# A graph network on one core: four chunks to a PSUM bank in the table products, and the last dense layers as one pipeline over groups of 512 nodes

## What is computed

```python
h = jnp.maximum(_layernorm(x, axis=-1), 0.0)
# the fourth layer, with x standing for h
h = jnp.concatenate([x[row], edge_attr], axis=1)
h = jax.nn.relu(h @ W1a + b1a) @ W1b + b1b
sums = jax.ops.segment_sum(h, col, num_segments=n_nodes)
counts = jax.ops.segment_sum(jnp.ones((h.shape[0],), dtype=h.dtype), col, num_segments=n_nodes)
agg = sums / jnp.clip(counts, 1.0)[:, None]
z = jnp.concatenate([x, agg, u[batch]], axis=1)
return jax.nn.relu(z @ W2a + b2a) @ W2b + b2b
```

## Time and profile before

| | us |
|---|---|
| median of 3 runs | 9367.44 (9365.83 to 9368.25) |
| the profiled execution, as timed | 9366.17 |
| its span | 9364.40 |

### The profile page before, as it was taken

One profiled execution on the slowest core, in us unless ns is written; L12 is line 12 of the kernel. 1 busy time (PEld: TensorE's weight loads), 2 busy tenths in 40 slices (PEclk: granted clock), 3 DMA queues, 4 the chain that ended last, 5 costly groups with the idle time before them and its releaser, 6 DMA issues. The chain is left out here.

```text
span 9364.4 us, 133857 instructions
## 1 busy us (share of the span) xinstructions
PE 7028.5 (75%) x35740; PEld 4596.9 (49%) x35792; DVE 5660.6 (60%) x16783; ACT 2515.7 (27%) x5863; POOL 2656.2 (28%) x2952
## 2 busy tenths in 40 slices
PE   4777777775566659940488699999998777777787
PEld 4555555453122224420477544444445666666676
DVE  6777777775589990059899800000014777777786
ACT  0222222222467740020388600000001333310001
POOL 0777777776470000000000000000002444444410
PEclk9767776766679989975799899999999999999998
DMA  3333333334975538849566478787886766642363
GB/s 99 103 103 105 105 104 103 105 105 167 393 231 164 168 114 306 299 195 426 205 215 216 144 262 276 262 287 256 295 284 200 181 180 179 179 111 63 63 178 88
DMA packets 969628, 1759.77 MB, mean 188 GB/s; under 512 B 102288, under 2 KB 665125, under 8 KB 905315
## 3 DMA queue, kind: packets, MB, share of 16 engines
q1 hardware_dynamic: 683820, 1335.73, 44.1%
q0 software_dynamic: 110720, 276.01, 9.0%
q10 hardware_dynamic: 174394, 139.51, 5.5%
HBM read 1412.04 MB, written 338.80 MB: 187 GB/s over the span
## 5 line engine op out<-in xcount | busy, mean ns | idle before, releaser
L768 POOL DMA_INDIRECT bucketed<-arena,wide x1563 | 1515.6, 970 | 726.5 <-issue 714.0
L1920 PE MATMUL psum<-wide,arena 128*128 x6496 | 1209.9, 329 | 400.5 <-DVE arena L1979 393.9
L1920 PEld LDWEIGHTS psum<-wide,arena 128*128 128x128 f32 x6496 | 989.9, 195 | 618.3 <-issue 493.3
L1787 POOL DMA_DIRECT2D table<-wide x13 | 9.7, 743 | 4316.2 <-DVE wide L1711 4316.2
L1979 DVE TENSOR_SCALAR arena<-wide,tile_first 128x128 f32 x3248 | 870.8, 300 | 472.3 <-PE psum L1920 293.8
L1841 POOL DMA_INDIRECT arena<-table,src_i x832 | 803.3, 966 | 1009.1 <-PE psum L1937 872.4
L1660 PE MATMUL psum<-arena,h 128*128 128x512 f32 (+1 forms) x2548 | 1048.6, 570 | 19.1 <-DMA arena<-adjacency 17.5
L922 PE MATMUL psum<-arena 128*128 128x512 bf16 x2253 | 695.7, 442 | 435.0 <-DVE arena L870 259.4
L665 PE MATMUL psum<-arena 128*113 128x177 bf16 x1568 | 534.4, 341 | 416.2 <-ACT wide L687 374.6
L870 DVE TENSOR_SCALAR arena<-sums 128x512 bf16<-128x512 int16 x2304 | 799.9, 347 | 0.0
L659 PE MATMUL psum<-w_edge,arena 128*128 128x256 f32 x1568 | 786.9, 597 | 0.0
(11 more groups left out here) (398 smaller groups left out, 11006.0 us busy)
## 6 DMA issues: line engine op xcount, KB each, us to landing
arena<-adjacency SPq DMA_DIRECT2D x294, 1024.0 KB
arena<-adjacency SPq DMA_DIRECT2D x98, 1568.0 KB, 7.8
adjacency<-wide SPq DMA_DIRECT2D x588, 256.0 KB
arena<-adjacency SPq DMA_DIRECT2D x196, 640.0 KB, 3.9
arena<-adjacency SPq DMA_DIRECT2D x147, 768.0 KB
arena<-bucketed POOLq DMA_DIRECT2D x208, 528.0 KB, 6.0
arena<-adjacency SPq DMA_DIRECT2D x49, 1792.0 KB, 6.9
arena<-adjacency SPq DMA_DIRECT2D x49, 1344.0 KB, 6.1
```

What stands on the lines that cost most here:

```text
L768: e.indirect_dma_start(bucketed, bass.IndirectOffsetOnAxis(ap=places[k][0:size, c:c + 1], axis=0), rows[k][0:size, c, :], None).then_inc(s ...
L1920: e.matmul(flat[:, ds((chunk & 3) * 512 + 2048, P)], lhsT=hot[:, i % 8, :], rhs=table_in[:, ds(tile * P, P)], start=False, stop=True, skip ...
```

## The change

1. **Split.** `NEAR_PAIRS` goes from 416 to 320, so far pairs from 416 to 512. `LOOKS` is 3048; a round has six lookups (`PER_PAIR`), and 508 of the 512 far pairs have one.
2. **Banks.** A PSUM bank holds four near chunks side by side, a quad; four banks hold sixteen chunks. ScalarE prepares and evicts a quad with one instruction each, 512 wide. Hots have sixteen slots. Sources are loaded eight chunks at a time.
3. **Rings.** Far gathers and far edge loads have four slots (`FAR`) instead of eight, the near block's loads four instead of eight.
4. **Tail inputs.** The third convolution also stores the turned nodes to DRAM (`nodes_t`), thirteen more transfers on GpSimd's queue. A row of flags, which node has an edge, is stored early. Both are fetched back (3.2 MB each into SBUF) on ScalarE's queue in the near block.
5. **Tail.** The three dense layers and the store are one pipeline over thirteen groups of 512 nodes (the last has 128). TensorE turns only the means; the first two layers' products have the weights as the stationary side and 512 columns of nodes. `b1b` and the flags are applied in one VectorE instruction, the rectifier reads PSUM and takes its bias on ScalarE, and each group is stored when its sum is ready.
6. The fold of `u` into the bias moves to the small steps behind the early scatter.

The core of the diff:

```diff
-NEAR_PAIRS = PAIRS // 2
+NEAR_PAIRS = 320
 NEAR = NEAR_PAIRS * PAIR
 FAR_PAIRS = PAIRS - NEAR_PAIRS
-LOOKS = -(-(NEAR + BUCKETS_49 + 2) // 16) * 16
+PER_PAIR = 6
+LOOKS = -(-(NEAR + BUCKETS_49 + 2) // PER_PAIR) * PER_PAIR
 MARKS = -(-LOOKS // P) * P
 NEAR_BLOCKS = -(-NEAR // P)
 DUMP = 4096
 PACK = 4096
 EARLY, LATE = 2560, 512
-PER_PAIR = 8
 QUAD = 4
+HOTS = 16
+FAR = 4
+NEAR_BANKS, ROW_QUADS, EDGE_QUADS = 4, 8, 3
+LIST_FROM = ROW_QUADS * QUAD
...
                             e.dma_start(table_nodes[:, a // P:(a + n) // P, :], wide2[:, a // P:(a + n) // P, :]).then_inc(s_saved, 16)
-                        e.wait_ge(s_saved, 16 * GROUPS)
+                            e.dma_start(nodes_t[:, a:a + n], part(wide, a, n)).then_inc(s_saved, 16)
+                        e.wait_ge(s_saved, 32 * GROUPS)
...
-            ring = slots(PAIR * P, DEEP).rearrange("p k (c w) -> p k c w", c=PAIR)
-            edge_in = slots(PAIR * P, DEEP).rearrange("p k (c w) -> p k c w", c=PAIR)
+            ring = slots(PAIR * P, FAR).rearrange("p k (c w) -> p k c w", c=PAIR)
+            edge_in = slots(PAIR * P, FAR).rearrange("p k (c w) -> p k c w", c=PAIR)
             onehot = slots(PAIR * P, 4).rearrange("p k (c w) -> p k c w", c=PAIR)
-            hot = slots(P, 8)
+            hot = slots(P, HOTS)
             stage = slots(QUAD * P, 2)
+            near_edge = slots(QUAD * P, EDGE_QUADS)
             tile_of = room(LOOKS).bitcast(i32)[0:1, :]
...
-                        if n >= DEEP:
-                            e.wait_ge(s_pe, n - DEEP + 1)
+                        k = n % FAR
+                        if n >= FAR:
+                            e.wait_ge(s_pe, n - FAR + 1)
...
+                    def prepare(q):
+                        if q == quads:
+                            e.copy(bank(q), zeros[:, :]).then_inc(s_clear, QUAD)
                             return
-                        if c % QUAD == 0:
-                            e.wait_ge(s_near_edge[g % 3], 16 * (g // 3) + 16)
-                            e.wait_ge(row_in[g % 4].sem, row_in[g % 4].at + 16 * (g // 4) + 16)
-                        e.copy(bank(c), near_edge[:, g % 3, c % QUAD * P:(c % QUAD + 1) * P]).then_inc(s_clear, 1)
-
-                    def evict(c, end):
-                        g = c // QUAD
+                        e.wait_ge(s_near_edge[q % EDGE_QUADS], 16 * (q // EDGE_QUADS) + 16)
+                        if q % 2 == 0:
+                            r = q // 2
+                            e.wait_ge(s_near_rows[r % (ROW_QUADS // 2)], 16 * (r // (ROW_QUADS // 2)) + 16)
+                        e.copy(bank(q), near_edge[:, q % EDGE_QUADS, :]).then_inc(s_clear, QUAD)
+                        if q + EDGE_QUADS < quads:
+                            e.wait_ge(s_clear, LIST_FROM - 1 + QUAD * (q + 1))
+                            load_edges(q + EDGE_QUADS)
...
+                    def evict(q, end):
                         e.wait_ge(s_looked, end)
-                        if c % QUAD == 0 and g >= 2:
-                            e.wait_ge(s_near_out[g % 2], 16 * (g // 2) + 16 * (g % 2 == 0))
-                        e.activation(stage[:, g % 2, c % QUAD * P:(c % QUAD + 1) * P], bank(c), ACT.Relu).then_inc(staged.sem, 1)
-                        e.wait_ge(staged.sem, staged.at + c + 1)
-
-                    e.sem_inc(s_clear, 15)
+                        if q >= 2:
+                            e.wait_ge(s_near_out[q % 2], 16 * (q // 2) + 16 * (q % 2 == 0))
+                        e.activation(stage[:, q % 2, :], bank(q), ACT.Relu).then_inc(staged.sem, 1)
+                        e.wait_ge(staged.sem, staged.at + q + 1)
...
+                    for q in range(quads):
+                        if q % 4 == 0:
+                            _, end = nc.values_load_multi_w_load_instructions(
+                                end_of[0:1, q * QUAD:(q + 4) * QUAD], engines=(ENG.Activation,), min_val=1, max_val=LOOKS,
+                                skip_runtime_bounds_check_because=reason)
+                        evict(q, end[q % 4 * QUAD + QUAD - 1])
+                        if q + NEAR_BANKS <= quads:
+                            prepare(q + NEAR_BANKS)
+                        e.dma_start(near_rows[:, q * QUAD * D:(q + 1) * QUAD * D], stage[:, q % 2, :]).then_inc(s_near_out[q % 2], 16)
+                        if q % 2 == 1 and q // 2 + ROW_QUADS // 2 < quads // 2:
+                            load_rows(q // 2 + ROW_QUADS // 2)
...
-                        e.matmul(flat[:, ds((chunk & 3) * 512 + 2048, P)], lhsT=hot[:, i % 8, :], rhs=table_in[:, ds(tile * P, P)],
+                        e.matmul(flat[:, ds((chunk & (NEAR_BANKS * QUAD - 1)) * P + 2048, P)], lhsT=hot[:, i % HOTS, :], rhs=table_in[:, ds(tile * P, P)],
                                  start=False, stop=True, skip_group_check=True).then_inc(s_looked, 1)
...
-                                if i >= 8:
-                                    e.wait_ge(s_looked, i - 6)
-                            e.tensor_scalar(hot[:, i % 8, :], rows[:, ds((chunk[k] & 15) * P, P)], tile_first[:, ds(tile[k], 1)], None,
+                                if i >= HOTS:
+                                    e.wait_ge(s_looked, i - HOTS + 2)
+                            e.tensor_scalar(hot[:, i % HOTS, :], rows[:, ds((chunk[k] & (ROW_QUADS * QUAD - 1)) * P, P)], tile_first[:, ds(tile[k], 1)], None,
...
+            quad_in = FAR
+            near_in = part(arena, 0, DEEP * PAIR * P).rearrange("p (k w) -> p k w", k=quad_in)
+            near_hot = part(arena, DEEP * PAIR * P, DEEP * PAIR * P).rearrange("p (k c w) -> p k c w", k=DEEP, c=PAIR)
...
+                @block.scalar
+                def _(e):
+                    e.dma_start(part(wide2, 0, NODES), nodes_t).then_inc(s_tail, 16)
+                    e.wait_ge(s_x, 48)
+                    e.dma_start(part(sums, 0, NODES), some_rows.rearrange("t p -> (t p)").unsqueeze(0).broadcast_to([P, NODES])).then_inc(s_tail, 16)
...
-        dense([(*mean_of_sums(), W["L3_gnn_W1b"])],
-              [("vector", lambda e, i, p: e.tensor_tensor(stage[1][:, :, :], row["L3_gnn_b1b"][:, :].unsqueeze(1).broadcast_to(tiles(BATCH)),
-                                                          s["some"][:, ds(i * BATCH, BATCH)].unsqueeze(2).broadcast_to(tiles(BATCH)), ALU.mult)),
...
+                    def turn_means(g):
+                        n = dst_groups[g][1]
+                        e.wait_ge(s_mean.sem, g + 1)
+                        if g >= 2:
+                            e.wait_ge(s_copied.sem, g - 1)
+                        for c in range(n // P):
+                            last = e.transpose(psum[:, g % 2, c * P:(c + 1) * P], means[g % 2][:, c * P:(c + 1) * P], ident[:, :])
+                        last.then_inc(s_turned.sem, 1)
+
+                    def aggregate(g):
+                        n = dst_groups[g][1]
+                        e.wait_ge(s_copied.sem, g + 1)
+                        if g >= 2:
+                            e.wait_ge(s_agg_done.sem, g - 1)
+                        e.matmul(psum[:, 2 + g % 2, 0:n], lhsT=W["L3_gnn_W1b"][:, :], rhs=turned[g % 2][:, 0:n], start=True, stop=True).then_inc(s_agg.sem, 1)
+
+                    def hide(g):
+                        a, n = dst_groups[g]
+                        if g >= 2:
+                            e.wait_ge(s_rectified, g - 1)
+                        e.matmul(psum[:, 4 + g % 2, 0:n], lhsT=W["h"][:, :], rhs=nodes_in[:, a:a + n], start=True, stop=False)
+                        e.wait_ge(s_agg_done.sem, g + 1)
+                        e.matmul(psum[:, 4 + g % 2, 0:n], lhsT=W["agg"][:, :], rhs=aggregated[g % 2][:, 0:n], start=False, stop=True).then_inc(s_hidden, 1)
+
+                    def finish(g):
+                        n = dst_groups[g][1]
+                        e.wait_ge(s_rectified, g + 1)
+                        if g >= 2:
+                            e.wait_ge(s_added, g - 1)
+                        for c in range(n // P):
+                            last = e.matmul(psum[:, 6 + g % 2, c * P:(c + 1) * P], lhsT=hidden[g % 2][:, c * P:(c + 1) * P], rhs=W["L3_gnn_W2b"][:, :],
+                                            start=True, stop=True)
+                        last.then_inc(s_out, 1)
+
+                    e.wait_ge(s_tail, 32)
+                    for i in range(GROUPS + 3):
+                        for stage_of, g in ((turn_means, i), (aggregate, i - 1), (hide, i - 2), (finish, i - 3)):
+                            if 0 <= g < GROUPS:
...
+                    def copy_turned(g):
+                        n = dst_groups[g][1]
+                        e.wait_ge(s_turned.sem, g + 1)
+                        if g >= 2:
+                            e.wait_ge(s_agg.sem, g - 1)
+                        e.copy(turned[g % 2][:, 0:n], psum[:, g % 2, 0:n]).then_inc(s_copied.sem, 1)
...
```

(22 more changed lines are left out.)

254 lines of the change are left out of this document (109 added, 145 removed).

## The result

| | before | after |
|---|---|---|
| median, us | 9367.85 (9365.83 to 9379.54, 4 runs) | 9878.26 (9875.51 to 9889.16, 4 runs) |
| ratio | | 1.0543 [1.0529, 1.0556] |
| span of the profiled execution, us | 9364.4 | 9876.0 |

What follows compares the result with a forecast made beforehand. The prediction took TensorE's sequencer, with its register loads and lookups in order, to bound the far rounds. Far -99, near -48, tail -85 and elsewhere +5 gave -227, so 9139 (median 9140), range 9080 to 9260 us.

Steps and rivals of the forecast that it cites:

- The bound: Far rounds: TensorE's sequencer runs two register loads 1.18, lookups 2.87 and the rest 0.18 in order, 4.23 us.
- The step that failed: Far rounds: six-value register loads would take 0.453 us each, 0.91 for both, in a TensorE round of 3.25.
- the eight-value loads become 0.45 us: Far rounds: sign to look for in the trace, together with start to start of 3.25 to 3.4 us.
- Register loads don't shrink: Rival in the far rounds: loads of six cost as eight, +142 us, 9282; chance 0.04.
- No slack: Rival in the far rounds: two engines without slack, 3.5 us a round, +86, 9226; chance 0.14.
- VectorE's waits for ScalarE's bank copy nearly gone: Sign in the live far rounds: the 91.8 us of waits for prepared banks, 0.36 a round, should go.
- The gather ring: Far stretch: four slots instead of eight cost nothing, 1.9 us a round hidden under 3.3; rival of starved gathers, chance 0.05.
- Near: Near pairs: 320 instead of 416, 195.3 us plus 10 for large loads, 205 in all, -48.
- The 10 us for the large loads at the entry: Near stretch: fetching turned nodes and flags beside near loads costs 10 us, the middle between nothing and 21.
- Tail: Dense layers and store: 4.20 us a group on TensorE, 51.4 for all, 63 with extras, -85 us.
- the clock rival: Rival: clock stays down in the tail, +43, and near loads stall, +11, 9194; chance of clock or near loads 0.11.
- Elsewhere: Other parts: thirteen more GpSimd stores +2 us, small relay steps behind the scatter +3, together +5.

Runs made afterwards that it cites:

- before_off8: The kernel before with both lookup lists moved by two values (8 bytes) in SBUF; 11376.79 us against 10261.35 (one run).
- load12: The changed kernel with one register load of twelve values serving two rounds of six; far stretch 1794.1 us.
- best12: The changed kernel with twelve-value loads for two rounds, eight near load slots, early flags and turned nodes in thirteen pieces; 9177.17 us, ratio 0.9797 of before.
- slot8: The changed kernel with each round's six values in a list place of eight, so all loads start on a boundary; far stretch 2085.6 us.
- alt84: The changed kernel with rounds of eight and four lookups in turn instead of six; 10224.14 us, ratio 0.9972 of before.
- split416: The changed kernel with the old split and round (416 near pairs, eight lookups); far stretch 1792.5 us.
- gather8: The changed kernel with eight gather slots again instead of four; far stretch 2437.8 us.
- best84: The changed kernel with rounds of eight and four, eight near load slots, early flags and turned nodes in thirteen pieces; 10237.64 us, ratio 0.9961 of before.
- dram_last: The twelve-value-load kernel with gentler near entry, its new DRAM buffers declared behind near_rows; 9199.25 us (one run).

## Why the prediction was wrong, point by point

**The bound was right.** The prediction put the round on TensorE's sequencer: two register loads, the lookups, the rest. The kernels above follow that sum with their measured loads in the padding: 4.64 for 4.65 (after), 6.93 for 6.89 (before_off8), 3.19 for 3.33 to 3.41 (load12, best12); slot8's 3.98 stands against 4.05 for all its rounds. One rival the runs don't part: VectorE loads the same two lists at nearly the same prices, and every edit changed both engines. For TensorE speak the sums, and the constant step from its second load to its next lookup.

**The step that failed** is one sentence: "An eight-value load is 0.592, ScalarE's four-value load 0.314, 0.07 a value, so 0.453 each". Two points, at four and eight values, both on a 16-byte boundary, were joined by a line, and six read off in between. They were points of a stair of groups of four, and 24-byte steps leave the boundary every second time. The mechanism, two loads in order on TensorE's sequencer, was right; this term of the sum was mis-sized. TensorE's two loads measured 1.17 and 1.21 on average (single long ones included), 2.38 a round and not 0.91, which is 750 us over 508 rounds. The 0.03 to 0.13 a round that the forecast had put on top, 41 us, did not come, as TensorE's queue was now the longer one by far. What is left, 709 us, matches the 712 by which the far stretch missed its 1717. The sign forecast for it, "the eight-value loads become 0.45 us", fails in the first row of the changed kernel's source lines.

**The rival that named this place was priced wrongly.** "Register loads don't shrink" was bounded at the eight-value price, with 0.04, and dismissed by the four-value row. That fewer values could cost *more* was left out. And rows were to be had. The trace of before has loads of other lengths (source lines of thirteen values on ScalarE's queue, and of seven on SyncE's), which the prediction doesn't use:

```profile
L940 ACTq TENSOR_LOAD <-wide x49: 1000/3137/3693, 2269.9 to 3392.2; - x49
```

```profile
L405 SPq TENSOR_LOAD <-last_i x4: 1141/2249/2856, 154.4 to 173.0; - x4
```

Thirteen values in 3.14 us are 0.24 each, 1.0 at best; at 0.07 a value it would be 0.9 always. In order of time every fourth of these 49 loads is a short one (1.00 to 1.56, the others 2.84 to 3.69), as steps of 52 bytes reach a 16-byte boundary every fourth time. This row alone allowed 1.44 for six values and a round of 2 x 1.44 + 2.34 = 5.2: 508 of them are 2650 us, and the whole is slower.

**No slack** (the first rival) is right beside the main error, in the versions with short loads: 0.14 to 0.22 a round above TensorE's own sum in the padding, where the forecast had 0.03, and 0.25 to 0.35 in live rounds (3.44 in best12, 3.54 in load12), where it had 0.13. It was priced at 3.5 a round; alt84 ran at 3.48.

**"VectorE's waits for ScalarE's bank copy nearly gone"** held in split416 (5.4 us) but not in the changed kernel, whose view still puts 78.0 us in 38 waits to the bank copies. A register load of VectorE's that ended last would be put down in the same way; the runs don't show which it was.

**The gather ring** fell as a cause (gather8); that nothing would wait was right but for the drain, where pairs without lookups follow each other.

**Near: right, the term a third too small.** -42.6 for -48. The 10 us for the large loads at the entry was 15.2 (210.5 less 195.3). In best84 and best12 it is gone; they both take the large loads away from the entry and give the near loads eight slots again, so the two runs alone don't say which of the two did it. The traces do say that the near loads were held up. The timeline of the changed kernel, its first products; the earlier trace rows has the first one 2.7 us behind the stretch's start, here it is 10.2:

```profile
9603.57 2.08 PE L1978 MATMUL psum<-arena 128*128 128x128 f32 x8 [10.90 <-DMA arena<-near_rows]
...
9612.96 7.68 PE L1978 MATMUL psum<-arena 128*128 128x128 f32 x48 [7.31 <-DMA arena<-near_rows]
```

The DMA queues of its first 21.6 us (packets, MB, share of the engines' time), and of the 16 us from 9595 to 9611 by themselves; q10 is the nodes and flags, q1 the near loads:

```profile
DMA packets 1002, 7.72 MB, mean 358 GB/s; under 512 B 111, under 2 KB 111, under 8 KB 746
...
q10 hardware_dynamic: 288, 6.42, 73.4%
q1 hardware_dynamic: 714, 1.30, 18.8%
...
q10 hardware_dynamic: 249, 5.85, 88.9%
q1 hardware_dynamic: 249, 0.48, 9.1%
```

The near loads got 60 GB/s (1.30 MB in 21.6 us) where they need 217. At that rate 21.6 x (217 - 60)/217 = 15.6 us are lost, the measured 15.2. Of the two bounds, "near loads stand still for 21 us" was the nearer one; the middle had no row.

The Trainium skill (DMA: Bandwidth & Descriptors, Queues, rings and completion order) says that an engine takes a packet from each queue in turn. The trace agrees, if one counts packets and not bytes: while both queues had work, from 9595 to 9611, each had 249 packets. But q10's hold 23 KB each and q1's 1.9 KB, so that the near loads had 30 GB/s of 395, and not half. The 13 us that the prediction worked out assumed halves, and that assumption was wrong.

**Tail: right, 9 us short.** -75.8 for -85: 72.1 for 63. The last group of 512 nodes and the entry of the next in the changed kernel's timeline:

```profile
9858.00 0.66 PE L2034 MATMUL psum<-ident,arena 128*128 128x128 f32 x4 [1.38 <-DVE arena L2096]
...
9861.07 1.05 PE L2058 MATMUL psum<-w_L_gnn_W2b,arena 128*128 128x128 f32 x8
...
9862.16 0.69 DVE L2116 TENSOR_TENSOR x<-x,psum 128x512 f32<-128x512 f32 x1 [1.26 <-PE psum L2058]
9862.76 0.28 DVE L2096 TENSOR_TENSOR arena<-h,s_rcount 128x128 f32<-128x128 f32 x1
...
9863.10 0.33 PE L2034 MATMUL psum<-ident,arena 128*128 128x128 f32 x1 [0.98 <-DVE arena L2096]
```

From the turns to the end of the last product are 4.12 us, the 4.20 of the forecast. Then TensorE waits. VectorE's four steps were called hidden by their sum, 2.7 a group, but its queue has an order: the mean of the next group (L2096) stands behind the residual (L2116), which waits for this group's last product (L2058). The waits in the tail (us in total, times, longest) give the price:

```profile
PE psum L2034 <- DVE arena L2096: 17.0, 12, 2.6
```

Of these 17 us the forecast had set aside 3 for a slow clock and 3 for the entry; the 11 that are left cover the missing 9. The last store is issued at 9872.25 and the span ends at 9876.0, 3.75 for the forecast 3.5; the clock was 0.96, so the clock rival had no part.

**Elsewhere:** +17 for +5 on the first chip, +1.5 (7156.9 against 7155.4) with best12 on chip 2 and +22 with dram_last there. The same part moves by 20 us from one build to the next, so the forecast's 5 can't be told from nothing.

## What to carry to other kernels

Where an engine's sequencer bounds a loop, count its register loads, and cost a load by length *and* address from a row with that length and that address; a load of an odd length elsewhere in the same trace can already show the rule. A price read off between two measured sizes is a guess, and its other side must be bounded too: here six values cost more than eight. Where a batch size must change, keep its start in the list on a 16-byte boundary and its length a multiple of four values, or load for several rounds at once (best12), and before calling a step hidden by its sum, ask what stands ahead of it in its queue.

## What was not expected of the hardware

- Register loads go in groups of four values: 0.314 us for four (ScalarE), 0.592 for eight, 0.849 for twelve on a 16-byte boundary; 0.82 for six on it; 1.48 (TensorE) and 1.42 (VectorE) for six off it; 1.94 and 1.85 for eight off it; 3.14 for thirteen off it (ScalarE). Off the boundary means 8 bytes off for six and eight values; other offsets were seen only with thirteen. Every value outside a full group on a boundary costs about 0.24.
- Single loads took up to 1.4 us even on a boundary (the largest of L1926 before; 1.55 in alt84), and almost only in the live stretch: of the kernel before's 1014 loads there on the two engines 92 took over 0.95 us, of the 610 in the padding one. What holds them is open.
- Two DMA queues with work took turns by packet, 249 to 249 in 16 us. Beside packets of 23 KB the other queue's loads, in packets of 1.9 KB, fell to 30 GB/s, a thirteenth of the traffic. Half of those bytes (the nodes) in thirteen pieces behind the near loads, on the same queue, cost nothing that can be seen (near 194.1 against 195.3).
- The same far stretch ran within 0.2% on two chips (2429.4 and 2433.1), and the part ahead of it 14% apart (7164.0 and 8146.9).
